# Three moves in the hand-written order of one attention kernel's matmuls and reductions

## The reference

```
h = _layernorm(x, axis=-1) * (1 + ca) + sa
qkv = x @ qkv_w + qkv_b
local = _local_attention(heads(q), heads(k), heads(v))
...
lscores = jnp.einsum('bhsd,bhld->bhsl', rq, rk) * lscale
lattn = jax.nn.softmax(lscores, axis=-1)
lat_out = jnp.einsum('bhsl,bhld->bhsd', lattn, rv)
remote = lat_out @ rout_w + rout_b
gate = jax.nn.sigmoid(local @ gl_w + remote_h @ gr_w)
mixed = gate * local + (1.0 - gate) * remote_h
return mixed @ out_w + out_b
```

## Time and profile before

| what | value |
|---|---|
| three runs | 574.83, 575.29 and 580.44 us, median 575.29 us |
| profiled execution | 574.33 us |
| its span, first to last instruction | 572.6 us |
| mean granted TensorE clock | 0.946 |
| busy share of the span | PE 85%, DVE 76%, POOL 66%, PEld 64%, ACT 61% |

### The profile page before, as it was taken

One profiled execution on the slowest core, in us unless ns is written; L12 is line 12 of the kernel. 1 busy time (PEld: TensorE's weight loads), 2 busy tenths in 40 slices (PEclk: granted clock), 3 DMA queues, 4 the chain that ended last, 5 costly groups with the idle time before them and its releaser, 6 DMA issues.

```text
span 572.6 us, 19855 instructions
## 1 busy us (share of the span) xinstructions
PE 487.8 (85%) x7168; PEld 367.4 (64%) x7168; DVE 436.1 (76%) x1193; ACT 348.5 (61%) x868; POOL 379.1 (66%) x516
## 2 busy tenths in 40 slices
PE   2535879899799989999999899999999899988661
PEld 2304557677577767777777677677777677766441
DVE  2156645988589978888889888888899688877554
ACT  1211465677577756677677667777777676666530
POOL 2222345777578758877788688777787587756663
PEclk9977889999899989999999999999999899989875
DMA  9558743707444453426171717171625344440000
GB/s 277 116 138 249 172 99 63 160 30 190 71 94 94 95 93 76 95 67 110 49 137 39 151 38 144 37 148 39 134 56 118 69 99 90 94 67 10 11 10 19
DMA packets 56523, 55.15 MB, mean 96 GB/s; under 512 B 7380, under 2 KB 53100, under 8 KB 54892
## 3 DMA queue, kind: packets, MB, share of 16 engines
q1 hardware_dynamic: 53564, 52.57, 41.4%
q10 hardware_dynamic: 2864, 1.31, 1.1%
HBM read 37.07 MB, written 16.80 MB: 94 GB/s over the span
## 4 chain that ended last, share of the span: by engine, by line
PE 64%; issue 13%; POOL 9%; DVE 6%; ACT 4%; DMA 2%; ACTq 1%; SPq 1%; POOLq 0%; DVEq 0%
PE p_pv L818 8%; PE p_qkv L730 8%; PE p_qkv L740 6%; PE p_misc L884 5%; PE p_y L805 4%; PE p_x L785 4%; PE p_y L806 4%; PE p_x L778 4%; PE p_a L751 3%; POOL pr L441 2%; PE p_a L830 2%; PE p_misc L867 2%; PE p_qkv L858 2%; PE p_a L716 2%; POOL pr L445 2%
## 5 line engine op out<-in xcount | busy, mean ns | idle before, releaser
L592 ACT ACTIVATE pr<-p_y 128x512 f32<-128x512 f32 x224 | 122.5, 595 | 56.7 <-PE p_y L806 55.9
L1158 DVE TENSOR_REDUCE mtok<-p_x 128x3 bf16<-128x480 f32 (+1 forms) x192 | 109.3, 585 | 30.5 <-PE p_x L785 28.8
L441 POOL TENSOR_SCALAR_AFFINE_SELECT pr<-pr 128x512 f32<-128x512 f32 x128 | 89.5, 700 | 10.7 <-ACT pr L594 6.8
L451 POOL TENSOR_TENSOR rstd<-ve,half 128x1 f32<-128x1 f32 x96 | 58.3, 607 | 47.9 <-DVE ve L1078 47.7
L469 POOL TENSOR_TENSOR dif<-local,rem 128x272 f32<-128x272 f32 x32 | 30.9, 966 | 81.7 <-DVE local L1196 81.7
L445 POOL TENSOR_SCALAR_AFFINE_SELECT pr<-pr 128x512 f32<-128x512 f32 x112 | 81.9, 732 | 0.0
L806 PE MATMUL p_y<-qst,kst 112*128 112x128 bf16 x512 | 73.1, 220 | 1.0 <-ACT qst L583 1.0
L805 PE MATMUL p_y<-qst,kst 112*128 112x128 bf16 x448 | 67.1, 222 | 7.4 <-ACT pr L592 4.8
L818 PE MATMUL p_pv<-pr,vp 128*18 128x128 f32 x1920 | 67.5, 281 | 2.4 <-issue 1.1
L730 PE MATMUL p_qkv<-hT,wqk 128*128 128x256 f32 x256 | 66.1, 403 | 2.2 <-DVE qkf L1110 1.3
L583 ACT ACTIVATE qst<-p_pv 16x2048 bf16<-16x2048 bf16 x32 | 59.8, 1870 | 10.1 <-PE p_pv L794 9.6
(11 more groups left out here) (131 smaller groups left out, 1099.6 us busy)
## 6 DMA issues: line engine op xcount, KB each, us to landing
scr_q<-terms SPq DMA_DIRECT2D x16, 384.0 KB, 2.6
qst<-scr_q SPq DMA_DIRECT2D x16, 384.0 KB, 4.7
scr_k<-terms SPq DMA_DIRECT2D x16, 384.0 KB, 4.4
kst<-scr_k SPq DMA_DIRECT2D x16, 384.0 KB, 5.4
qst<-scr_q SPq DMA_DIRECT2D x16, 256.0 KB, 5.4
kst<-scr_k SPq DMA_DIRECT2D x16, 256.0 KB, 6.4
out_y<-y SPq DMA_DIRECT2D x32, 128.0 KB, 1.9
x_all<-in_x SPq DMA_DIRECT2D x3, 1024.0 KB, 8.3
```

The source lines that it names most:

```text
L441: ins = pool.affine_select(out=own, in_=own, compare_op=ALU.is_ge, fill=0.0, base=-1, pattern=[[0, 4], [1, P]], channel_multiplier=-1)
L592: act.activation(pr[:, 2 * i:2 * i + 2, :, :], src, ACT.Exp).then_inc(exp_done[i], 1)
L1158: dve.tensor_reduce(mtok[:, t % 2, KS + h0:KS + h1], p_x[i % 2][:, 0:(h1 - h0) * w].rearrange("p (h n) -> p h n", n=w), AX_X, ALU.max, neg ...
```

## The change

No instruction is added or removed; three groups of them change their place in the lists of PE and DVE.

On PE, `max_t` moves behind `scores(t, 0)` and `lat_scores`, `project_v` moves ahead of `scores(t, 3)`, `scores(t, 2)` moves up to just behind `scores(t, 3)`. Late in the slot `mixed_t` moves ahead of `scores(t, 4)` and `lat_p_t`, these two change places, and `project_out` moves ahead of all four value products. On DVE `copy_v` moves ahead of `norm1`, and `maxima(t, 2)` moves up between `prob_sum` and the steps that lead to `local`.

```diff
 if S:
     scores(t, 1)
-if T:
-    max_t(m)
-if S:
     scores(t, 0)
     lat_scores(t)
 if T:
+    max_t(m)
     lat_out_t(m)
+if K:
+    project_v(k)
 if S:
     scores(t, 3)
-if K:
-    project_v(k)
+    scores(t, 2)
 if T:
     scores_t(m, 1)
 if C:
     out_tokens(c)
 if T:
     scores_t(m, 0)
-if S:
-    scores(t, 2)
...
 if T:
     scores_t(m, 7)
     scores_t(m, 6)
-if S:
-    lat_p_t(t)
-    scores(t, 4)
 if C:
     mixed_t(c)
-if T:
-    sum_v(m, 1)
+if S:
+    scores(t, 4)
+    lat_p_t(t)
 if C:
     project_out(c)
 if T:
+    sum_v(m, 1)
     sum_v(m, 3)
     sum_v(m, 2)
     sum_v(m, 0)
...
     maxima(t, 0)
+if K:
+    copy_v(k)
 if A:
     norm1(a)
 if S:
     maxima(t, 3)
-if K:
-    copy_v(k)
 if C:
     prob_sum(c)
+if S:
+    maxima(t, 2)
...
     maxima(t, 5)
-    maxima(t, 2)
```

## The result

The changed kernel took 584.68 us (median of 4 runs, 581.08 to 588.19), the kernel before 576.53 us in the same comparison: 1.0166 of its time, interval 1.0118 to 1.0214, that is 1.2 to 2.1% slower. A ratio here leaves out executions in the kernel's slow state and is not simply the quotient of the two medians. The profiled execution took 581.08 us with a span of 579.3 us, 6.7 us more than before; the mean granted clock was 0.944 against 0.946.

The account below looks back on a forecast made before the run. PE was taken to set the pace, busy 14.56 of 15.08 us in a usual slot. 23 slots at 0.42 (9.7 us) plus 2.8 us for seven late slots, 12.5 on 574.33, gave 586.8, stated as 587.0; range 570 to 601.

Parts of the forecast that it names:

- The wait of `max_t` goes, and most of what PE wins is asked back by later waits: Early in PE's slot: the 0.52 us wait on ACT's copy goes, only 0.20 is left at `project_lat`.
- "A group of three heads 0.40 us": PE's score matmuls early in the slot: each group of three heads costs 0.40 us from start to start.
- `shift` 0.21 later on ACT: ACT early in the slot: `shift` waits for the moved `max_t` and starts 0.21 us later, delaying the steps behind it.
- "I use this price for the slots with fewer latents too": All 23 slots with the wait on ACT's copy: each 0.42 us longer, 9.7 us together.
- "I take 401.06, near" ACT's bound: `project_out`'s start: between 400.93 and 401.42 by DVE's `mix`, taken as 401.06, near the 401.00 set by ACT's `mixT`.
- The lost cover: Late in PE's slot: the first value product no longer covers ACT's work to `mixT`, a new 0.56 us wait before `project_out`.
- The 7 late slots lose 0.4 each: Seven slots starting late for the transfer of queries and keys: +0.4 us each, 2.8 us together.
- The bound of -0.3: Lower end of the effect per slot starting late for a transfer: between -0.3 and +1.1 us.
- "The filling and draining slots I cost at nothing": Slots where the pipeline fills and drains: no cost, since both orders wait there.
- The clock did not fall: Rival: several short PE waits per slot lower the granted clock; 15 us more in half the slots, 602 us; chance 0.13.
- The faster rival: `max_t`'s wait goes and nothing takes its place: the 11.7 us are won, 562.6 us; chance 0.09.
- The even exchange: Rival: ACT and DVE have more slack, `project_lat` comes 0.52 us earlier, slot +0.04 us, about 578 us; chance 0.20.

Follow-up runs that it names:

- e10: Kernel before with only the change's early PE moves and earlier `copy_v`, keys and queries also changing places: 553.42 us, ratio 0.9624.
- e13: Changed kernel with `maxima(t, 2)` back behind `maxima(t, 5)`, keys and queries also changing places: 561.67 us, ratio 0.9784.
- e2: Changed kernel with DVE's `maxima(t, 2)` back behind `maxima(t, 5)`, PE order as changed: 575.58 us, ratio 1.0028.
- e0: The changed kernel run again, unedited: 584.45 us, ratio 1.0157 to the kernel before.
- e4: Kernel before with only the late part of PE's slot reordered as in the change: 580.85 us, ratio 1.0091.
- e1: Changed kernel with the late part of PE's slot put back as before: 580.19 us, ratio 1.0085.
- e11: Changed kernel, whole, with keys and queries changing places: 570.30 us, ratio 0.9914.
- The swap: Edit tried in four kernels: even stage projects, stores and loads keys, odd stage queries; on the kernel before 558.68 us, ratio 0.9731.
- e3: Changed kernel with both PE's late order and `maxima(t, 2)` put back, leaving the early PE moves and `copy_v`: 575.54 us, ratio 1.0004.

## Why the prediction was right, and where not

The direction and the range were right, the size only within a factor of two: 12.5 us were forecast for the profiled execution (586.8), and 6.7 came (581.08). (With the median's 0.96 the prediction's own sum is 587.8; it says 587.0.) That it came no further off is in part luck, since terms that were too dear and terms that were left out partly cancelled. By its own steps:

- *The wait of `max_t` goes, and most of what PE wins is asked back by later waits*: right, and shown by e10 to e13. PE's idle time in the middle grew by 11.9 us. I had not counted what PE itself wins there, 8.5 us, the better clock of the late slots included; a usual slot shows 0.27.
- *"A group of three heads 0.40 us"*: this is the term that was mis-sized. It was read from a group with another kind of matmul behind it. Two groups in a pair cost 0.29 to 0.30 for the first, `max_t` at its new place 0.05 instead of 0.15 (391.35 to 391.40), and the value products together 1.76 instead of 1.88. So the slot was 15.21 us, not 15.50: `project_out` came 0.13 earlier than reckoned (12.43 us behind the first scores, 12.56 forecast), and what follows it up to the next slot was 0.16 shorter (2.78, 2.94 forecast).
- *`shift` 0.21 later on ACT*: it started 1.49 us behind the first scores, 1.39 before, so 0.10 later; the pair made the difference. `project_lat` came 6.63 us behind the first scores (7.03 before, 6.83 forecast). PE waited for ACT's `modulated` there (0.19 us from the last transposed score to `project_lat`, 0.05 before), but that started 5.68 us behind the first scores, not 5.95: 0.11 earlier through `shift`, and 0.16 because I had counted the two `exps` ahead of it to their recorded end (1.12 us), while it began 0.96 behind their start (394.83 to 395.79). `ln_t` waited 0.32 where I had said about 0.1.
- *"I use this price for the slots with fewer latents too"*: one price does not fit them all. A usual slot lost 0.13 us where 0.42 were forecast, while the three slots in the middle that had taken 13.77 us lost 0.65 each.
- *"I take 401.06, near" ACT's bound*: the wrong one of the two bounds that I had. `mix` was late by 0.16, inside the 0.1 to 0.59 I had for it (`local` by 0.17, below the 0.3 to 0.6 I had named as a sign), and since PE was early, DVE alone set `mixed_t`, with a wait of 0.61. e2 shows that this comes from the moved reduction: 0.30 us a slot, 8.9 us in all against e0. The lost cover, which I priced at 0.56, is a wait of 0.44 us (e4), or 0.39 from the last transposed score to `project_out` (e2), and in the changed kernel it hides behind DVE's wait, as e1 shows.
- *The 7 late slots lose 0.4 each*: wrong in sign for the slots that started late before. The wait fell from 11.1 to 7.1 us in 6 slots, and by the starts of `project_out` the seven late slots of the middle were 3.0 us shorter together, 0.4 each. The bound of -0.3 was too narrow, since it left out the clock: the three of them that lost most time to it, at a mean of 0.90 to 0.91 before, ran at 1.00 in the changed kernel and were 1.35 to 1.37 us shorter each. Against that, two slots start late only in the changed kernel (waits of 1.13 us at 301.35 and 0.60 us at 481.46) and are 2.5 us longer together, which no term of the sum has.
- *"The filling and draining slots I cost at nothing"*: wrong; draining cost 3.9 us. The new waits at L875 are longest there (1.69 us in two slots running), and the granted clock falls behind them as it did before, to a mean of 0.84 in these slots against 0.88. In windows late in the span, which answer to the earlier trace rows:

```profile
507.00:509.00 2.00, 1.19 (x15) 0.61 (x16) 1.73 (x5) 0.38 (x1) 2.00 (x4) 0.68 1.20 163
509.00:511.00 2.00, 2.00 (x6) 1.42 (x6) 1.35 (x2) 0.39 (x1) 1.12 (x2) 0.50 0.17 23
```

- *The rivals.* The clock did not fall in the usual slots: waits of 0.32 and 0.61 in 15.21 us left it at 1.00. The Trainium skill ("TensorE: Matmul & The Clock Gate", section "A second HAM failure mode: psum-queue depth-cycling") tells of such a swing with short idle times between groups; the trace agrees in the drain only. The faster rival failed because something did take the wait's place. The even exchange would need ACT and DVE to be early. e2, where DVE is, comes out even in total (1.0028), but not by that sum: its usual slot is 0.17 us shorter than before, and the late slots take it back.

What stays open: e11 to e13 tell the parts apart only added in one order, and `copy_v` ahead of `norm1` was not tried by itself. The swap also puts each load right behind its store in the queue's list, ahead of the store of the output; the two were not tried apart. Why a group of matmuls costs less ahead of its like is not shown.

## What to carry to other kernels

In this slot PE, ACT, DVE and a transfer all stood close to the limit. The head of the change was worth 0.44 us a slot on PE, and by itself it won nothing in total (e3), since the transfers took it back; in the whole change DVE's order and PE's own tail took it back as well. With the transfers out of the way it counted (e10). Follow the chain to the next late engine, and of a reduction that is moved up ask what now stands behind it on its engine. When a gain per slot does not arrive in the total, look at the waits that no engine releases: here the order in which two loads were issued was worth more (17 us) than any of the orders of matmuls that were tried.

## What the hardware showed that was not expected

- The cost of a group of matmuls depends on its neighbour: the same sixteen matmuls (L778 and L785) took 0.29 to 0.30 us ahead of their like and 0.40 to 0.41 ahead of another kind.
- A store of 384 KB that shared the time with the other load landed in 4.4 us (median), with the loads a slot apart in 2.5. The transfers of the kernel before, then of e10 (KB each, median us to landing):

```profile
scr_k<-terms SPq DMA_DIRECT2D x16, 384.0 KB, 4.4
```

```profile
scr_k<-terms SPq DMA_DIRECT2D x16, 384.0 KB, 2.5
```

- A wait of PE of 1.95 or 2.92 us in an otherwise full slot came with a lower granted clock that cost another 1.7 us in that slot. Waits of 0.32 and 0.61 us in one slot left the clock at 1.00, and so did one of 2.56 us in the changed kernel, so what makes the difference stays open.
